# Pair 1 of a 20-product block multiplication in plain f32 instead of split f32r

## The reference

```
w  = L0_weights[cond]                            # 128 x 128 per sequence
x  = x + einsum('bct,bcd->bdt', x, w)
H  = einsum('btd,od->bto', x, W)                 # 1024 x 1024, the same for all sequences
xa = einsum('btd,brd->btr', x, A[adapter])       # rank 16
d  = einsum('btr,bor->bto', xa, B[adapter]) * scalings[adapter]
x  = x + H + d
```

## Time and profile before

| what | value |
|---|---|
| median of 3 runs | 783.86 us (782.89 to 784.75) |
| the profiled execution | 783.24 us, a span of 781.3 us from first to last instruction |
| TensorE (PE) busy | 758.3 us, 97% of the span |
| VectorE (DVE) busy | 620.7 us, 79% |
| ScalarE (ACT) busy | 509.2 us, 65% |
| GpSimd (POOL) busy | 191.7 us, 25% |
| mean granted clock of TensorE | 0.993 of full speed |

### The profile page before, as it was taken

One profiled execution on the slowest core, in us unless ns is written; L12 is line 12 of the kernel. 1 busy time (PEld: TensorE's weight loads), 2 busy tenths in 40 slices (PEclk: granted clock), 3 DMA queues, 4 the chain that ended last, 5 costly groups with the idle time before them and its releaser, 6 DMA issues.

```text
span 781.3 us, 16842 instructions
## 1 busy us (share of the span) xinstructions
PE 758.3 (97%) x4456; PEld 724.7 (93%) x4456; DVE 620.7 (79%) x1397; ACT 509.2 (65%) x1186; POOL 191.7 (25%) x428
## 2 busy tenths in 40 slices
PE   6996999999999999999999999999999999999997
PEld 3685999999999999999999999999999999999996
DVE  6999787987787887778887778798777788777864
ACT  3575667766666766666766666776666676666663
POOL 5621122221122222122222112222212222211200
PEclk9998999999999999999999999999999999999998
DMA  8432444233434323434423343433333432344222
GB/s 301 150 129 88 139 125 147 93 113 123 141 121 148 113 95 121 141 127 141 139 92 121 121 145 121 148 103 105 121 141 121 148 127 85 121 136 140 69 89 81
DMA packets 47140, 98.26 MB, mean 126 GB/s; under 512 B 6548, under 2 KB 26004, under 8 KB 47124
## 3 DMA queue, kind: packets, MB, share of 16 engines
q1 hardware_dynamic: 46706, 97.73, 37.3%
q10 hardware_dynamic: 418, 0.35, 0.2%
HBM read 63.45 MB, written 34.60 MB: 125 GB/s over the span
## 4 chain that ended last, share of the span: by engine, by line
PE 88%; DVE 6%; POOL 2%; DMA 2%; issue 1%; ACT 1%; SPq 0%; ACTq 0%; POOLq 0%; DVEq 0%
PE bank L1272 74%; PE o_ps L1309 4%; PE bank L1287 4%; PE o_ps L1308 4%; PE o_ps L1310 4%; DVE w_lo_raw L1100 1%; DVE w_lo L837 1%; DVE x_lo L837 1%; DMA s_tab<-scalings 1%; DMA a_now<-lora_a 1%; POOL w_hi_raw L432 1%; DVE z_lo L837 1%; DVE c_sb L840 0%; POOL w_lo_raw L432 0%; DVE x_raw L837 0%
## 5 line engine op out<-in xcount | busy, mean ns | idle before, releaser
L1272 PE MATMUL bank<-w_hi,x_hi 128*128 128x342 f32 (+1 forms) x1240 | 404.7, 326 | 7.1 <-DVE x_lo L837 3.2
L1272 PE MATMUL bank<-w_lo,x_hi 128*128 128x342 f32 (+1 forms) x1240 | 400.5, 323 | 0.0
L1272 PE MATMUL bank<-w_hi,x_lo 128*128 128x342 f32 (+1 forms) x1240 | 399.8, 322 | 0.0
L1272 PEld LDWEIGHTS bank<-w_hi,x_hi 128*128 128x128 f32 x1240 | 233.8, 189 | 17.7 <-DVE x_lo L837 3.5
L1272 PEld LDWEIGHTS bank<-w_lo,x_hi 128*128 128x128 f32 x1240 | 233.7, 188 | 3.0
L1272 PEld LDWEIGHTS bank<-w_hi,x_lo 128*128 128x128 f32 x1240 | 234.2, 189 | 0.0
L837 DVE TENSOR_TENSOR x_lo<-x_raw,x_hi 128x256 fp32r<-128x256 f32 (+1 forms) x279 | 150.6, 548 | 32.9 <-ACT x_hi L484 28.3
L484 ACT ACTIVATE x_hi<-x_raw 128x256 fp32r<-128x256 f32 (+1 forms) x279 | 138.2, 507 | 59.0 <-PE bank L1272 47.9
L292 POOL TENSOR_TENSOR w_lo<-a_ride,w_hi 128x160 fp32r<-128x160 f32 x31 | 16.2, 522 | 516.5 <-ACT w_hi L484 516.5
L484 ACT ACTIVATE c_sb<-bank 128x342 f32<-128x342 f32 x190 | 85.4, 451 | 40.7 <-PE bank L1272 40.6
L484 ACT ACTIVATE z_hi<-c_sb 128x340 fp32r<-128x340 f32 (+1 forms) x128 | 60.5, 490 | 54.5 <-DVE c_sb L840 54.5
(11 more groups left out here) (85 smaller groups left out, 842.9 us busy)
## 6 DMA issues: line engine op xcount, KB each, us to landing
x_raw<-xT SPq DMA_DIRECT2D x64, 512.0 KB, 5.1
out<-o_sb SPq DMA_DIRECT2D x62, 512.0 KB, 2.8
b_stack_raw<-b_split SPq DMA_DIRECT2D x128, 128.0 KB, 2.5
a_now<-lora_a SPq DMA_DIRECT2D x64, 64.0 KB, 3.3
c_raw<-cond_w SPq DMA_DIRECT2D x64, 64.0 KB, 1.8
w_lo_raw<-wB SPq DMA_DIRECT2D x7, 342.0 KB, 6.6
w_hi_raw<-wB SPq DMA_DIRECT2D x4, 342.0 KB, 6.9
out<-x_raw SPq DMA_DIRECT2D x4, 256.0 KB, 2.0
```

The lines of the kernel that those rows point to most:

```text
L1272: last = nc.tensor.matmul(bank[:, lo:hi], x[:, left, c * C:(c + 1) * C], w[:, c, FIRST[o]:FIRST[o] + WIDTH[o]], start=opens and c == 0 and ...
```

## The change

Pair 1 is computed with the same 20 products, but in plain f32, as pair 0's dense products are: two matmuls a product, on the unsplit sums of weights (in w_lo_raw) and on unsplit left operands, taken from x_raw[1] or from a new tile x_whole, which lies in the memory of x_hi and holds the ten sums. So pair 1 needs no upper and lower parts. Those of the left operands are first made for pair 2. The upper parts of the weights are still made during pairs 0 and 1. The lower parts of 17 and 13 stay where they were; the other 18 overwrite the sums that pair 1 reads, so each waits for a product of pair 1 (`split_after`): twelve stand in VectorE's list of pair 1, and those of 16, 1, 3, 19, 6 and 12 in that of pair 2, whose step is written out for it. Therefore the loops of VectorE and TensorE begin one i later.

Other edits: the semaphores of left operands and rides begin at pair 2; GpSimd copies the rides of pair 1 unsplit into w_lo_raw (after the dense product of b10 is done); ScalarE's and VectorE's lists of pairs 0 and 1 are put in a new order; SP loads x of pair 3, which goes into x_raw[1], after product 12 of pair 1; the first transfers are exchanged (x of sequence 0 before b12 on SP, adapter index and scalings before b01 on ScalarE's queue).

The core of the diff:

```diff
+    WHOLE_SUMS = ("u_0", "u12", "v", "u_1", "u", "u910", "u67", "u11", "u54", "u3")
...
+            x_whole = sb("x_whole", [P, 18, W2], f32, plain)
...
-        ride_hi_ready = sem("ride_hi_ready", 1)
-        ride_ready = sem("ride_ready", 1)
+        ride_hi_ready = sem("ride_hi_ready", 2)
+        ride_ready = sem("ride_ready", 2)
...
-        hi_ready = {o: sem(f"{o}_hi_ready", 1) for o in OPERANDS}
-        lo_ready = {o: sem(f"{o}_ready", 1) for o in OPERANDS}
+        hi_ready = {o: sem(f"{o}_hi_ready", 2) for o in OPERANDS}
+        lo_ready = {o: sem(f"{o}_ready", 2) for o in OPERANDS}
...
+            load_x(0, 0, 0, 0)
             load_w(sp, "b12")
-            load_x(0, 0, 0, 0)
...
-            after(sp, lo_ready["u54"], 0, 1, 0)
-            after(sp, lo_ready["a02"], 0, 1, 0)
-            after(sp, lo_ready["u3"], 0, 1, 0)
+            sp.wait_ge(product_done["12"], 1)
             load_x(0, 1, 2, 0)
...
-            step(0, 0)
+            pick_scalings(0, 0, 1)
+            make_rides(pool, nc.gpsimd, 0, 0, 1)
+
+            dense_through(pool, "b10")
+            pool.wait_ge(a_summed, 4)
+            nc.gpsimd.tensor_copy(left_rides(w_lo_raw), rides(0, 5)).then_inc(whole_rides_ready, 1)
+            nc.gpsimd.tensor_copy(right_rides(w_lo_raw), rides(5, 4)).then_inc(whole_rides_ready, 1)
...
+            take_b(0, 0)
+            hi_of_c(0, 0)
+            made(act, "7")
+            in_place("7")
+            made(act, "11", "e")
+            dense_through(act, "b20")
+            in_place("11")
             turned_xa(0, 0, 0, 1)
             turned_xa(0, 0, 0, 0)
...
+            def split_after(o, done):
+
+                dve.wait_ge(product_done[done], 1)
+                in_place(o)
...
-            in_place("5")
-            in_place("15")
...
-            in_place("2")
...
-            in_place("0")
...
+            made(dve, "i10")
+            add("7", slot("lo", "7"), w_block("b10"), w_block("b12"), ALU.subtract)
...
+            whole("u_0", plus, x_whole[:, U, :], raw(0, 1)[:, 0, 0, :], raw(0, 1)[:, 0, 3, :])
+            whole("u12", subtract, x_whole[:, U1:U6, :], twice(raw(0, 1)[:, 1, 2, :]), outer_two(raw(0, 1)[:, 1, :, :]))
+            whole("v", plus, x_whole[:, U11, :], raw(0, 1)[:, 1, 1, :], raw(0, 1)[:, 1, 3, :])
...
+            split_after("5", "5")
+            sum_u12(0, 1, 1)
+            begin_u(0, 1, 1)
+            split_after("15", "15")
+            go_on_u(0, 1, 1)
+            split_after("2", "2")
+            end_u(0, 1, 1)
...
+            split_after("8", "8")
+
+            i, j = 1, 0
+            rest_a001(i, j, 0)
+            rest_z("12", i, j, -1)
+            rest_a03(i, j, 0)
+            sum_c01(i, j, -1)
+            sum_u54(i, j, 0)
+            rest_z("00", i, j, -1)
+            rest_z("01", i, j, -1)
+            sum_c02(i, j, -1)
+            rest_u54(i, j, 0)
+            split_after("16", "16")
+            rest_z("02", i, j, -1)
+            split_after("1", "3")
+            split_after("3", "3")
+            sum_u12(i, j, 1)
+            split_after("19", "19")
+            begin_u(i, j, 1)
+            rest_a02(i, j, 0)
+            go_on_u(i, j, 1)
+            split_after("6", "6")
...
+            split_after("12", "12")
+            rest_a13(i, j, 1)
+            sum_xa1(i, j)
...
+            step(1, 1)
+            run_steps(dve, step, 2)
...
+            def whole_product(o, bank, opens):
+
+                x, lo, hi = whole_left(LEFT[o]), BANK0[o], BANK0[o] + WIDTH[o]
+                for c in range(2):
+                    w = {"17": w_block("b12"), "13": slot("hi", "19")}.get(o, w_lo_raw[:, :, FIRST[o]:FIRST[o] + WIDTH[o]])
+                    last = nc.tensor.matmul(bank[:, lo:hi], x[:, c * C:(c + 1) * C], w[:, c, :],
+                                            start=opens and c == 0, stop=c == 1, skip_group_check=not opens)
+                return last
+
             def multiply(o, role, i, j, opens=False):
                 if not exists(i, j, -1, 1):
+                    if o != "17":
+                        made(pe, {"13": "s", "15": "v", "8": "y"}.get(o, o))
+                    return whole_product(o, bank_of(j, 0, role), opens)
+                if not exists(i, j, -1, 2):
                     pe.wait_ge(w_ready, SPLITS.index(o) + 1)
                 return product(o, bank_of(j, 0, role), opens)
...
             step(0, 1)
-            run_steps(pe, step)
+            step(1, 0)
+            step(1, 1)
+            run_steps(pe, step, 2)
```

More of the change, by code:

```diff
@@ L190, in cond_resid_kernel, with run_steps @@
         block = ctx.enter_context(nc.Block())
-        def run_steps(eng, step):
-            with eng.Fori(1, NP // 2 - 1) as i:
+        def run_steps(eng, step, first=1):
+            with eng.Fori(first, NP // 2 - 1) as i:
                 step(i, 0)
@@ L1331, in step @@
             def step(i, j):
-                after(pe, lo_ready["u11"], i, j, 0)
+                left("u11", i, j)
                 after(pe, c_block["11"], i, j, -1)
@@ L1336, in step @@
                     loras0(i, j, -1)
-                after(pe, lo_ready["u"], i, j, 0)
+                left("u", i, j)
+                if not exists(i, j, -1, 1):
+                    pe.wait_ge(whole_rides_ready, 2)
                 after(pe, ride_ready, i, j, 0, 2)
@@ L1341, in step @@
                 after(pe, c17_ready, i, j, 0)
-                after(pe, lo_ready["u910"], i, j, 0)
+                left("u910", i, j)
                 multiply("15", "beta", i, j).then_inc(product_done["15"], 1)
@@ L1350, in step @@
                 after(pe, c10_begun, i, j, 0)
-                after(pe, lo_ready["u12"], i, j, 0)
+                left("u12", i, j)
                 multiply("2", "beta", i, j).then_inc(product_done["2"], 1)
@@ L1366, in step @@
                 after(pe, c12_begun, i, j, 0)
-                after(pe, lo_ready["u54"], i, j, 0)
+                left("u54", i, j)
                 multiply("9", "beta", i, j).then_inc(product_done["9"], 1)
@@ L1373, in step @@
                 turn1(i, j)
-                after(pe, lo_ready["u3"], i, j, 0)
+                left("u3", i, j)
                 multiply("16", "pi12", i, j).then_inc(product_done["16"], 1)
@@ L1378, in step @@
                 after(pe, c02_begun, i, j, 0)
-                after(pe, lo_ready["a001"], i, j, 0)
+                left("a001", i, j)
                 multiply("1", "alpha", i, j)
@@ L1385, in step @@
                 multiply("3", "alpha", i, j).then_inc(product_done["3"], 1)
-                after(pe, lo_ready["a02"], i, j, 0)
+                left("a02", i, j)
                 after(pe, c_block["12"], i, j, -1)
@@ L1393, in step @@
                 multiply("6", "beta", i, j).then_inc(product_done["6"], 1)
-                after(pe, lo_ready["a03"], i, j, 0)
+                left("a03", i, j)
                 if exists(i, j, 1):
```

312 lines of the change are left out of this document (158 added, 154 removed).

## The result

The changed kernel takes 779.74 us (median of 4 runs, 779.56 to 779.92), the kernel before 784.03 beside it (4 runs, 782.89 to 784.75): the ratio is 0.9947, with a 95% interval of 0.9935 to 0.9960. That is 4.3 us less, where 8.2 were forecast; it lies in the predicted range and beside rival (b) (780.5), not beside the forecast. The profiled execution took 779.57 us, with a span of 777.8 us and a mean granted clock of 0.998.

The account below looks back on a forecast made before the run. VectorE was taken to bound pair 1 and the head of pair 2, TensorE the steady state. Gain 8.6 at product 13 of pair 2 less 0.4 stall is 8.2, from 783.86 to 775.7 us; range 772.2 to 780.2.

Parts of the forecast that it names:

- rival (b): VectorE further behind: product 13 of pair 2 at 75.4, 2.0 us of stall, gain 3.4, 780.5 us; chance 0.20.
- TensorE's part: Pair 1: plain products cost 1.15 or 1.20 us against 0.94 or 0.99 split, 4.2 us more TensorE work.
- The floor: TensorE's earliest start of product 13 of pair 2, 70.2, counted from product 17 of pair 1 at 38.8.
- The gap before the adapter products: Pair 0, TensorE at 37.46: its 1.28 us wait for ScalarE's copies was taken as gone.
- VectorE's part: Sum of block 01 before product 13 of pair 2: from 79.41 to 70.8 (bounds 68.7 and 74.0).
- the term for waits and contention: VectorE before the sum of block 01: added wait for GpSimd less vanished waits and contention, +1.7 us (-0.4 to +4.9).
- What is late next: Pair 2: six put-off VectorE splits, 4.7 us, make the adapter sum late; 0.4 us of stall (0 and 2.0).
- At nothing: Effects priced at zero, among them pair 1's seed of product 10 behind u's upper part, covered by VectorE's chain.
- The exchange of the first transfers: Start of the dense products at 7.48: moves by some 0.9 us at most, taken as nothing.
- What pair 1 lost before: Pair 1 and the head of pair 2 lose 13.5 us, read as TensorE waiting for VectorE.
- (c): The work only moves: added wait 4.9, six put-off splits return as stalls of pair 2; gain 0.7, 783.1 us; chance 0.03.
- Rival (d): Slower clock after TensorE starves at product 10 of pair 1: ten products cost 12 us more, 787.7 us; chance 0.05.

Follow-up runs that it names:

- e8: Changed kernel with each product of pair 1 leaving out its second chunk of 128 rows, one plain matmul instead of two; 780.58 us (one run).
- e6: e5 plus pair 1's seed of product 10 ahead of u's upper part and eight unused matmuls in TensorE's last wait; 775.88 us.
- e12: e6 with the first transfers back in their old order; 774.57 us.
- e1: Changed kernel with, in ScalarE's list of pair 2, the bank-opening copies and adapter rows ahead of the upper part of u; 777.10 us.
- e2: Changed kernel with, in VectorE's list of pair 2, the sums of u ahead of the splits of 16, 1, 3, 19 and 6; 776.68 us.
- e3: Changed kernel with only two of pair 2's five splits (19 and 6) put behind u on VectorE; 778.05 us.
- e10: Changed kernel with the first transfers back in their old order; 780.48 us.
- e4: Changed kernel with, on ScalarE in pair 0, c's upper part ahead of the adapter rows and the adapter-sum copies ahead of 7 and 11; 778.36 us.
- e7: Kernel before the change with only the first transfers exchanged; 785.46 us, ratio 1.0018.
- e9: Changed kernel with eight matmuls that nobody reads in front of TensorE's last wait; 780.00 us.
- e5: Changed kernel with the edits of e2 and e4 together; 775.05 us.

## Why the prediction was wrong

- **TensorE's part** held. Products of 342 columns begin 1.15 apart (48.13, 49.28), two of 358 take 56.39 - 53.98 = 2.41, 1.205 each, as the rows of pair 0 had given. The Trainium skill ("FP8 and Floating Point Precision", section "TensorE Precision Notes") gives true FP32 four passes through the array. The estimate worked out from that, 4/3 of a split product and 2.1 us more, is not what the rows show, which is 1.15 against 0.94, or 1.22. e8, with half of these matmuls, ended the stretch no sooner, so that neither price decided. The floor itself, 31.4 us from 17 of pair 1 to 13 of pair 2, was reached by no run: the shortest way is 33.6 (e6, e12).
- **The gap before the adapter products** (1.28 us, taken as gone) stayed, at 1.26, in the profiled execution. The landing was predicted well, 33.4 against 33.38. But TensorE came 1.2 us sooner than before, so it met the same copies as early as ever. That depends on where it starts: with the same order on ScalarE, but dense products from 8.69 to 8.80 on, e1, e2 and e3 have no such gap. Product 17 of pair 1 began at 39.15, not 38.8. Since VectorE set the stretch, these 0.35 us cost nothing.
- **VectorE's part** was right in kind and 1.4 us short: the sum of block 01 came at 72.21, within its bounds, not at 70.8. With 5.6 removed and 4.7 moved, the term for waits and contention came out at 3.1 and not 1.7. Part of it can be told apart in e10, whose sum 5 stands at 10.29 as in the kernel before: from there to the sum of block 01 VectorE is idle for 6.67 us instead of 2.57, and busy for 11.3 less, where 10.3 had been worked out. Of the waits I had seen only the one for GpSimd, and too large (1.43 us in the changed kernel, not up to 5.4). The one for c, 2.25 us, I had not seen: I followed the adapter rows to TensorE's gap, and not to the operation that stands behind them on the same queue and feeds VectorE. e4 removed it and had 0.9 to 1.0 us of the sum back.
- **"What is late next" is the step that failed.** It took 0.4 us (0 to 2.0) for the six splits put off, and looked for their lateness at the adapter sum of pair 2, where there is room. There VectorE was not late: at 86.06 it still waited 0.74 for TensorE. The splits were late at u, a few operations earlier in the same list, and through the seed of product 10 on ScalarE: 2.6 us, over the bound. e1, e2 and e3 show the chain link by link. The neighbouring sentence, under "At nothing", named the very same chain, seed behind the upper part of u, for pair 1, where it cost 0.93, and found it covered by VectorE; in pair 2 nothing covered it, since behind 13 of pair 2 TensorE sets the time.
- **The exchange of the first transfers**, taken as nothing with up to 0.9 us of gain, is a loss of 1.4 us by itself (e7), which delays VectorE more than TensorE. In the changed kernel it is hidden (e10).
- **The end**, not in the sum, took 0.96 us more in the profiled execution, because the granted clock fell ahead of the last six matmuls (0.43 apart), and in the kernel before only among the last of them.
- **What pair 1 lost before**, 13.5 us, was read as TensorE's waits alone. It is idle for 40.72 - 31.99 = 8.7 of them; a part of the rest, some 3 us by estimate (0.08 of 40.72), is the lower clock in the same row. No term of the sum hangs on this.

The sum now reads 775.7 + 1.4 for VectorE + 2.3 for the stall (2.70 less 0.4) + 0.96 for the end - 0.45, because the median lies only 0.17 over the profiled execution and not 0.62: 779.9, against 779.74. Rival (b) named the right two terms with other sizes (13 at 75.4, measured 73.61; stall 2.0, measured 2.7); that its time comes so near is partly luck, since the one is 1.8 too much, the other 0.7 too little, and the end is not in it. Of (c) the part "splits come back as stalls" holds in half: 2.6 of 4.7. Rival (d), the clock at product 10 of pair 1, did not come: its wait was 0.93 and the clock stayed at 1.00. Where e8 made this wait 4.69 us, the granted clock behind it was 0.50 (52.52 to 56.50). In the changed kernel the long wait came at the same product of the next pair. The Trainium skill ("TensorE: Matmul & The Clock Gate", section "HAM oscillation — how this bites in real kernels") warns that idle gaps bring the lower level back; behind this wait of 2.6 us three profiles agree (e8, e9, e10), and those of the changed kernel and of e4 don't, so the wait decided it only in part.

What stays open: in which executions the level falls behind such a wait, or at the end, was not controlled; nor was the start of the dense products, which with the exchanged transfers lies between 7.22 and 8.91 in the profiles.

## What to carry to other kernels

Work that is put off must be followed on every queue that reads behind it. Find the first operation behind it that another engine waits for, then list what stands behind that operation on the other engine, ready or not: here five subtractions of 0.78 us cost 2.6 us through a copy that needed none of them, and moving that copy or the sum ahead of them won it back. Before an earlier start is counted as a gain, look for the next wait whose end is set by something else; 1.5 us of head start vanished in one of 3.77 us.

## What was unexpected of the hardware

The same wait of TensorE, 2.6 us at the same place of the program, was followed by the upper clock level in two profiles (the changed kernel and e4, 24 matmuls in 4 us) and by about ten matmuls 0.30 apart, instead of 0.16, in three others (e8, e9, e10): 1.3 to 1.5 us more. Behind the last wait of 2.2 us the changed kernel lost 0.96 us more than the kernel before in the same way, while the last six matmuls of e1, e2, e4 and e5 stayed at the upper level. The four runs of the changed kernel agree within 0.4 us, those of e9 and e10 spread over 2.2 to 2.6, so a single run is no measure of an edit worth one microsecond here.
